# Cross-attention and BitLinear FFN: another order of loads, projections, squares and last steps

## The reference, cut to what matters

```
q = LN(x) @ Wq.T + bq;  k = ctx @ Wk.T + bk;  v = ctx @ Wv.T + bv
a = softmax(q k.T / 4, masks) @ v
x = x + a @ Wo.T + bo
h = gelu(silu(bitlinear(LN(x), w1, b1)))          # 512 -> 2048
h = (h - mean(h)) * rsqrt(var(h) + eps) * g + b
x = x + bitlinear(h, w2, b2)                      # 2048 -> 512
bitlinear(x, w, b): x rms-normed, scaled to +-127 per token and rounded; w -> {-1,0,1} * mean|w|
```

## Time and profile before

| stretch, us | what runs | PE | DVE | ACT | PE clock |
|---|---|---|---|---|---|
| 0 to 42 | start, up to the first score | 26.31 | 22.52 | 11.04 | 0.99 |
| 42 to 62 | first pass of batch 0 | 17.97 | 18.30 | 7.66 | 0.86 |
| 62 to 91 | body 0, second pass | 20.14 | 18.19 | 16.64 | 0.76 |
| 91 to 111 | body 0, first pass of batch 1 | 15.60 | 18.13 | 2.32 | 0.87 |
| 111 to 163 | body 1 up to its first pass | 41.52 | 29.06 | 26.27 | 0.85 |
| 189 to 436 | bodies 2 to 5 | 237.40 | 219.04 | 166.20 | 1.00 |
| 436 to 475 | body 6 up to its first pass | 31.25 | 32.84 | 23.28 | 0.87 |
| 498 to 552 | body 7 | 42.02 | 36.15 | 31.13 | 0.87 |
| 552 to 580 | body 8, first part | 20.79 | 23.08 | 21.84 | 1.00 |
| 580 to 621 | bodies 8 and 9, end | 25.37 | 28.60 | 10.82 | 0.75 |

### The profile page before, as it was taken

One profiled execution on the slowest core, in us unless ns is written; L12 is line 12 of the kernel. 1 busy time (PEld: TensorE's weight loads), 2 busy tenths in 40 slices (PEclk: granted clock), 3 DMA queues, 4 the chain that ended last, 5 costly groups with the idle time before them and its releaser, 6 DMA issues.

```text
span 620.8 us, 8914 instructions
## 1 busy us (share of the span) xinstructions
PE 524.9 (85%) x3374; PEld 289.5 (47%) x3374; DVE 489.0 (79%) x728; ACT 350.8 (57%) x424; POOL 135.0 (22%) x101
## 2 busy tenths in 40 slices
PE   4778497689889999999999999999869969698446
PEld 4666133362456355645564556455425523343222
DVE  3769939349699978997899789988896887648784
ACT  0244280517584867486748674867187739287630
POOL 5030031100611061106110611301140113103220
PEclk9989598797989999999999999999969989799688
DMA  8588637934422641365136412642134221100000
GB/s 315 152 234 324 211 84 191 386 116 146 86 67 105 183 99 36 125 195 114 36 124 191 102 54 76 191 98 74 40 86 102 74 75 17 38 0 1 34 34 35
DMA packets 32994, 72.17 MB, mean 116 GB/s; under 512 B 7167, under 2 KB 14529, under 8 KB 29950
## 3 DMA queue, kind: packets, MB, share of 16 engines
q1 hardware_dynamic: 31798, 71.26, 38.8%
q10 hardware_dynamic: 1152, 0.31, 0.2%
HBM read 46.50 MB, written 20.61 MB: 108 GB/s over the span
## 4 chain that ended last, share of the span: by engine, by line
PE 58%; DVE 12%; DMA 10%; ACT 9%; issue 7%; SPq 2%; POOL 1%; ACTq 1%; DVEq 0%
PE FF L853 9%; PE FF L678 7%; PE PV L792 7%; PE FF L901 6%; ACT PT L1069 5%; PE PV L775 5%; PE S L759 5%; PE S L735 5%; DVE negm L1337 4%; PE S L888 3%; PE FF L855 2%; PE PV L735 2%; DMA work<-in_w 2%; PE FF L867 2%; DMA num<-o_raw 2%
## 5 line engine op out<-in xcount | busy, mean ns | idle before, releaser
L1069 ACT ACTIVATE PT<-S 128x1024 f32<-128x1024 f32 x128 | 123.6, 1033 | 28.1 <-PE S L759 28.0
L1337 DVE TENSOR_REDUCE negm<-S 128x4 f32<-128x1024 f32 x88 | 105.6, 1215 | 24.7 <-PE S L735 23.2
L759 PE MATMUL S<-Q,K 100*128 100x512 bf16 x256 | 78.0, 413 | 27.7 <-ACT PT L1069 18.3
L775 PE MATMUL PV<-PT,vaug 128*32 128x256 f32 x1024 | 71.8, 400 | 0.4 <-ACT PT L1069 0.4
L853 PE MATMUL FF<-w1t,xqT 128*128 128x512 bf16 x256 | 67.4, 386 | 2.0 <-ACT PT L1100 1.1
L1100 ACT ACTIVATE work<-FF,s 128x512 f32<-128x512 f32 x56 | 38.5, 687 | 40.6 <-PE FF L855 40.6
L792 PE MATMUL PV<-wo_sb,num 128*128 128x512 f32 x128 | 59.9, 614 | 0.4 <-DVE negm L1337 0.4
L678 PE MATMUL FF<-xnT,wq_sb 128*128 128x256 f32 x224 | 52.8, 394 | 8.6 <-ACT xnT L1039 8.6
L735 PE MATMUL S<-K,Q 97*128 97x256 bf16 x352 | 54.5, 282 | 6.6 <-issue 3.5
L759 PEld LDWEIGHTS S<-Q,K 100*128 100x128 bf16 x256 | 18.7, 101 | 77.4 <-ACT PT L1069 54.8
L1337 DVE TENSOR_REDUCE negm<-PV 128x4 f32<-128x1024 f32 x40 | 48.8, 1221 | 6.3 <-PE PV L735 5.9
(11 more groups left out here) (196 smaller groups left out, 858.5 us busy)
## 6 DMA issues: line engine op xcount, KB each, us to landing
Q<-q_d SPq DMA_DIRECT2D x15, 768.0 KB
work<-in_w SPq DMA_DIRECT2D x8, 1024.0 KB, 11.4
q_d<-part SPq DMA_DIRECT2D x8, 768.0 KB, 3.6
x_sb<-in_x SPq DMA_DIRECT2D x8, 512.0 KB, 4.0
ctx_sb<-in_ctxT SPq DMA_DIRECT2D x8, 512.0 KB, 4.0
q_d<-part SPq DMA_DIRECT2D x8, 512.0 KB, 3.3
xb_sb<-in_x SPq DMA_DIRECT2D x8, 512.0 KB, 3.9
rec<-rec_d SPq DMA_DIRECT2D x30, 128.0 KB, 2.6
```

The lines of the kernel that those rows point to most:

```text
L759: last = pe.matmul(where, K[0:ROWS_2, g, kt * P:(kt + 1) * P], Q[0:ROWS_2, g, 2 * pair:2 * pair + 2, :], start=not masked, stop=True)
L775: last = pe.matmul(PV[32 * r:32 * r + 32, g % 4, :], vaug[:, c % 2, kt, g, :], PT[:, n % PT_SLOTS, r, :], start=(kt == 0), stop=(kt == TT ...
L1069: act.activation(PT[:, n % PT_SLOTS, :, :], ST[n % 2][:], ACT.Exp, scale=0.25).then_inc(S["pt_made"], 1)
L1337: dve.tensor_reduce(negm[:, t, R * g:R * g + R], RING_1[n % 3][:], AX.X, ALU.max, negate=True).then_inc(S["max_made"], 1)
```

## The change

All edits are made together:

- **Start.** On PE `project_kv` is split; K(0) comes first, then x(0) is turned, then V(0). ACT takes `keys`, `turned_x` and `values_in` in that order and K no longer waits for bv's load. On DVE `key_rests(0)` moves ahead of `masks`, and the first `maximum` ahead of `key_rests(1)`. On SP x(1) goes ahead of the second context, w1's chunk 0 behind `key_parts(0)`, x(2) from ahead of `query_parts(0)` to behind `rows_back_first`, w1's chunks 1 to 3 behind x(2).
- **w2.** GpSimd issues the four chunks on its own queue, as soon as w1_done, ahead of `norm_1(3)`. The sum, mean and first two DVE passes of w2 move forward in body 1; the third stays.
- **Bodies.** On PE `project_out(f, 0)`, `turn_max`, `turn_x(w)`, `project_out(f, 1)`, `project_q(w)`, K(a), the first two `scores_2`, V(a). The V copy follows the second exponential. In body 6 `squares(t, 1)` follows the second exponential. SP's `rows_back(a, 1)` goes ahead of the last denominators and numerators. The mean is an ACT instruction behind each gelu.
- **End.** In body 7 both `squares` go behind exponentials, `turn_hq` uses S1 and S0 instead of FF and needs no eviction first, and DVE takes `maximum_2(t, 1)` ahead of `turn_1`. In body 8 all of `layer_1` runs ahead of `layer_2_last(6, 1)`. In body 9 `shift(t, 0)` comes ahead of `spread_last(t, 1)`.

```
+
+def turned_hq_ps(t, n):
+    where = S0w if t == B - 3 and n > 1 else S1w
+    return where[:, 512 * (n % 2):512 * (n % 2) + 512]
...
 def weight_sum_ps(n):
-    return PV[:, 0, 0:1] if n == 0 else FF[:, 1, 1:2]
+    return PV[:, 0, 0:1] if n == 0 else S1[:, 0, 0:1]
...
         sp.dma_start(work[:, cols], w[:, cols]).then_inc(S[f"w_chunk{n}"], 16)
-
-    weight_chunk(w1, 0)
-    weight_chunk(w1, 1)
...
 
-    def second_weights():
-        sp.wait_ge(S["w1_done"], 1)
-        for n in range(4):
-            weight_chunk(w2, n)
+    def layer_rows():
         for to, of in ((b2_bc, b2), (g_bc, ln_g), (b_bc, ln_b)):
             sp.dma_start(to[:], of.partition_broadcast(P)).then_inc(S["w_two"], 16)
...
         if at_start(a):
+            load_x(1)
             load_context(1)
-            load_x(1)
             key_parts(0)
-            load_x(2)
+            weight_chunk(w1, 0)
             query_parts(0)
             negatives()
             rows_back_first()
-            weight_chunk(w1, 2)
-            weight_chunk(w1, 3)
+            load_x(2)
+            for n in range(1, 4):
+                weight_chunk(w1, n)
             query_parts(1)
             key_parts(1)
             weights_and_biases()
...
             denominators(c, 2)
-            denominators(c, 3)
-            numerators(c, 1)
         if a is not None:
             rows_back(a, 1)
         if c is not None:
+            denominators(c, 3)
+            numerators(c, 1)
+        if c is not None:
             reciprocals(c)
         if at_start(c):
-            second_weights()
+            layer_rows()
...
+    def second_weights():
+        pool.wait_ge(S["w1_done"], 1)
+        for n in range(4):
+            cols = slice(2048 * n, 2048 * n + 2048)
+            pool.dma_start(work[:, cols], w2[:, cols]).then_inc(S[f"w2_chunk{n}"], 16)
...
-
-    def mean_3(f, t):
-        pool.wait_ge(S["gelu_made"], 2 * f + t + 1)
-        tt(st[:, 1, t:t + 1], st[:, 0, t:t + 1], cst("-1/inner", (P, 1)), ALU.mult, "mu_made")
...
+        if at_start(c):
+            second_weights()
         if w is not None and w + 1 < B:
             norm_1(w + 1)
             norm_1_apply(w + 1)
...
-    def weight_sum(n, a):
-        if n == 0:
-            pe.wait_ge(S["max_made"], 16)
-        else:
-            pe.wait_ge(S["k_made"], a + 1)
-            pe.wait_ge(S["r1k_made"], a + 1)
-            pe.wait_ge(S["v_placed"], a + 1)
+    def weight_sum(n):
+        pe.wait_ge(S["max_made"], 16 * n + 16)
         pe.wait_ge(S["w_sum"], n + 1)
         pe.matmul(weight_sum_ps(n), ones[:], wsum[:, n:n + 1], start=True, stop=True
...
-    def project_kv(a):
+    def project_k(a):
         if at_start(a):
...
         for k in range(KD):
-            pe.matmul(to[:, 0:T], wkv_sb[:, k, 0:P], ctx_sb[:, k, :],
-                      start=(k == 0), stop=(k == KD - 1))
+            last = pe.matmul(to[:, 0:T], wkv_sb[:, k, 0:P], ctx_sb[:, k, :],
+                             start=(k == 0), stop=(k == KD - 1))
+        last.then_inc(S["k_ps"], 1)
+
+    def project_v(a):
+        if a == 1:
+            pe.wait_ge(S["v_placed"], 1)
+        to = pair_of(a)
         for t in range(TT):
             for k in range(KD):
                 last = pe.matmul(to[:, 512 + t * P:512 + (t + 1) * P],
...
+        if n == 1 and c == 1:
+            pe.wait_ge(S["w_mean"], 4)
         if n >= 2:
...
-        pe.wait_ge(S["hqT_made"], 4 * t + n - 1)
+        if t > B - 3:
+            pe.wait_ge(S["hqT_made"], 4 * t + n - 1)
         for k in range(8):
-            last = pe.transpose(S1w[:, 512 * half:512 * half + 512].bitcast(BF16)[:, k * P:(k + 1) * P],
+            last = pe.transpose(turned_hq_ps(t, n).bitcast(BF16)[:, k * P:(k + 1) * P],
...
     def body_of(c, a, f, t, masked):
         w = next_front(a) if c != 0 else None
-        if w is not None:
-            turn_x(w)
         if f is not None:
             project_out(f, 0, c)
         if c is not None:
             turn_max(c)
+        if at_start(c) or at_start(f):
+            weight_sum(c)
+        if w is not None:
+            turn_x(w)
+        if f is not None:
+            project_out(f, 1, c)
         if w is not None:
             project_q(w)
-        if f is not None:
-            project_out(f, 1, c)
         if a is not None and a > 1:
-            project_kv(a)
-        if at_start(c) or at_start(f):
-            weight_sum(c, a)
+            project_k(a)
         for g in range(G + 1):
             if c is not None and g < G:
                 scores_2(c, 2 * g, masked)
                 scores_2(c, 2 * g + 1, masked)
+            if g == 0 and a is not None and a > 1:
+                project_v(a)
             if c is not None and g > 0:
                 values(c, 2 * g - 2)
...
             for n in range(4):
-                turn_hq(t, n, f)
+                turn_hq_last(t, n)
             for n in range(4):
-                layer_1(f, n, t)
+                layer_1(f, n, None)
             project_out(c, 0, None)
             project_out(c, 1, None)
             for n in range(4, 8):
-                layer_1(f, n, t)
+                layer_1(f, n, None)
             layer_2_last(t, 0)
         elif f is not None:
             turn_xq_last(f)
-            layer_1(f, 0, None)
-            layer_1(f, 1, None)
+            for n in range(8):
+                layer_1(f, n, None)
             layer_2_last(t - 1, 1)
...
-    project_kv(0)
+    project_k(0)
     turn_x(0)
+    project_v(0)
     project_q(0)
     mask_flag()
     turn_x(1)
     project_q(1)
-    project_kv(1)
+    project_k(1)
+    project_v(1)
...
 def _(act):
-    act.dma_start(bk_sb[:], bk).then_inc(S["w_bias"], 16)
+    act.dma_start(bk_sb[:], bk).then_inc(S["w_bk"], 16)
...
-    def keys_and_values(a):
-        act.wait_ge(S["kv_ps"], a + 1)
+    def keys(a):
+        act.wait_ge(S["k_ps"], a + 1)
         wait_for(act, S["k_out"], 48 * a)
         if at_start(a):
-            act.wait_ge(S["w_bias"], 48)
+            act.wait_ge(S["w_bk"], 16)
         act.activation(part[:, 0, R, :], pair_of(a)[:, 0:T], ACT.Identity, bias=bk_sb[:, 0:1]
                        ).then_inc(S["k_made"], 1)
+
+    def values_in(a):
+        act.wait_ge(S["kv_ps"], a + 1)
         if at_start(a):
...
                        ).then_inc(S["gelu_made"], 1)
+        act.wait_ge(S["gelu_made"], 2 * f + t + 1)
+        act.activation(st[:, 1, t:t + 1], st[:, 0, t:t + 1], ACT.Identity, scale=-1.0 / INNER
+                       ).then_inc(S["mu_made"], 1)
...
-            squares(t, 0)
             act.activation(table_call[:, 1:2], table_call[:, 0:1], ACT.Exp)
             for n in range(16):
                 exps(c, n)
-                if n == 3:
-                    squares(t, 1)
+                if n in (1, 3):
+                    squares(t, n // 2)
...
-            keys_and_values(0)
-            for b in range(2):
-                turned_x(b)
-                queries(b, 0)
-                queries(b, 1)
-            keys_and_values(1)
-            weight_abs_sum(0, range(2))
+            keys(0)
+            turned_x(0)
+            values_in(0)
+            queries(0, 0)
+            queries(0, 1)
+            turned_x(1)
+            queries(1, 0)
+            queries(1, 1)
+            keys(1)
+            values_in(1)
             turned_x(2)
-            weight_abs_sum(0, range(2, 4))
+            weight_abs_sum(0)
...
@@ -1185,16 +1195,20 @@
         if w is not None:
             queries(w, 0)
             queries(w, 1)
-        if t is not None and a is not None:
+        if t is not None and w is not None:
             squares(t, 1)
         if c is not None:
 
             act.activation(table_call[:, 1:2], table_call[:, 0:1], ACT.Exp)
         if a is not None and a > 1:
-            keys_and_values(a)
+            keys(a)
         if c is not None:
             for n in range(16):
                 exps(c, n)
+                if n == 1 and w is None and t is not None:
+                    squares(t, 1)
+                if n == 1 and a is not None and a > 1:
+                    values_in(a)
                 if n in (5, 9, 13):
                     values_out(c, (n - 5) // 4)
...
         maximum_2(t, 0)
         power_2(t)
+        maximum_2(t, 1)
         turn_1(f)
-        maximum_2(t, 1)
+        reciprocal_last(c)
         factor_2(t)
         scale_2(t)
-        reciprocal_last(c)
         normalise_last(c, 0)
         normalise_last(c, 1)
         for n in range(4):
-            turn_2(t, n)
+            turn_2_last(t, n)
...
+        maximum_2(t, 0)
         residual_2(t - 1, 1)
-        maximum_2(t, 0)
         power_2(t)
...
         gain(t, 0)
+        shift(t, 0)
         spread_last(t, 1)
-        shift(t, 0)
         gain(t, 1)
         power_last(t, 0)
...
             norm_1_apply(0)
+            key_rests(0)
             masks()
-            key_rests(0)
             norm_1(1)
             norm_1_apply(1)
             query_rests(0)
```

(29 more changed lines are left out.)

26 lines of the change are left out of this document (9 added, 17 removed).

## The result

The changed kernel took **625.46 us** (median of 20 runs, 620.92 to 628.69) against 621.76 for the kernel before on the same chips: ratio 1.0054, 95% interval 1.0031 to 1.0076. The forecast was 614, with 621 as its upper end.

The account below looks back on a forecast made before the run. TensorE was taken as full in bodies 2 to 5, with waits movable in the start, body 1 and bodies 6 to 9. Terms 9.1 + 1.2 - 10 - 2.1 - 5.0 - 1.9 = -8.7 gave 613.9 from 622.6 (614.0 by median), range 604 to 621.

Parts of the forecast that it names:

- step 3: Second half rows ahead of denominators 3: reciprocal waits 2 to 3 in body 0; +1.2 us, bounds -1.1 and +3.5.
- step 5: Bodies 2 to 5: TensorE's earlier work taken back by ScalarE; 0, bounds -1 and +1.5 over four bodies.
- step 7: Body 7: scaling and turns end 2.1 sooner, project_out(7) at 540, not 545.01; -5.0 us, bounds -3 and -7.
- step 4: w2 issued early by GpSimd, there before body 1, whose scores_2(1,0) comes sooner; -10 us, bounds -8 and -11.
- rival C: w2 lands late from GpSimd's queue and holds body 1; 629 from a landing at 128.6; chance 0.12.
- Step 1: Start: K, turning x and V back to back, so Q(0) starts at 15.8 instead of 18.33.
- Step 2: Start: new wait for x(2), first score at 48.4, last maximum 71.1; +9.1 us with Step 1's gain contained.
- Step 6: Body 6: exponential 0 need not wait for squares(t, 1), VectorE next holds turn_xq; -2.1 us, bounds 0 and -5.
- Step 8: Bodies 8 and 9: deviations(7, 1) no longer wait 3.40, late residual costs 0.4; -1.9 us, bounds 0 and -3.
- A: Start: x(2) lands 6.3 or less behind its issue; 611.7 or lower, to 605; chance 0.19.
- B: Start: x(2) lands 11.8 behind its issue, +3.2 us, 617.2; chance 0.15.
- D: Denominators late by 1 to 1.5 us in each of six bodies; 620 to 622; chance 0.07.

Follow-up runs that it names:

- g2: The changed kernel unaltered, run and profiled again: ratio 1.0040 to the kernel before, profiled at 623.66 us.
- f3: Changed kernel with w2's issue, project_out(f,1) and x(2) put back, plus last denominators and numerators ahead of rows_back(a,1): 0.9811 of the kernel before.
- g1: The same file as f3, run and profiled again: 0.9802 of the kernel before.
- e4: Changed kernel with project_out(f,1) behind project_q(w) again: 0.9967 of the kernel before.
- e7: Changed kernel with w2's issue, project_out(f,1) and x(2) put back, plus V beside K again: 0.9787 of the kernel before.
- e5: Changed kernel with SP's load of x(2) ahead of w1's first chunk and query_parts(0): 0.9921 of the kernel before.
- e2: Changed kernel with the four w2 transfers back on SP's queue at the end of body 0: 0.9900 of the kernel before.
- e8: Changed kernel with VectorE's residual_1(f,1) ahead of maximum_2(t,0) in every body: 1.0053 of the kernel before.
- g4: f5 with VectorE's residual_1(f,1) ahead of maximum_2(t,0), as in e8: 0.9667 of the kernel before.
- f5: Changed kernel with w2's issue, project_out(f,1) and x(2) put back, plus body 7's first two silus between the last numerators' issues: 599.90 us, 0.9662.
- e3: Changed kernel with w2 on GpSimd's queue held until batch 0's four denominators transfers have landed: 0.9948 of the kernel before.

## Why the prediction was wrong, by its own steps

The forecast said 614.0 and the median is 625.46. Of these 11.5 us, 6.9 lie in the stages of the table (−1.8 for −8.7), and 4.5 are the distance of the profiled run from its own median, of which g2's profile shows 2.8. The stages missed both ways: +7.7 in step 3, +4.3 in step 5 and +3.2 in step 7, against −8.4 in the others together, so that by luck the sum is nearer than its terms.

**Step 3 failed**: "it would wait 2 to 3 in body 0, where w2 shares the engines. Taken +1.2". The mechanism was named and the place was right; the size was 9.89 us of waiting and +8.9 in the stage, outside its bound of +3.5. The landing was priced by a row in which the queue had the engines to itself. The two halves of the mechanism stood in two different steps: w2's landing, taken in step 4 as anything up to 107.3 on the clock of the kernel before, was not laid over the denominators' issue, which by the same clock falls near 92. The rule of the Trainium skill that the text set beside rival C ("DMA: Bandwidth & Descriptors", "Queues, rings and completion order": engines take packets in turn from the queues that have work) made it say "w2 would slow SP's transfers of body 0 instead of being late itself". The traces agree with its first half: 13.3 us for 8 KB beside w2, and no wait over 0.51 without it. But w2 was slowed too: its last sum begins 23.8 us after the issue (86.80 to 110.58), where the chunks took 14.0 on SP's queue. It should have been a rival with a price. And the order itself is a gain: with w2 away it is worth 8 us (f3, g1), in part by a way that step 3 did not see, the 32 KB behind the rows.

**Step 5 failed**: "0, bounds −1 and +1.5". It counted how long each engine would take and not that K writes where Q(w)'s rests are still read. In the kernel before, the second project_out lay between the earlier trace rows; the change moved that cover away. Measured +4.3. In it are 1.93 of waiting per body, and 1.0 to 1.7 us in each body where the clock falls behind it (body 4 takes 64.13 from project_out to project_out, body 3 62.45; body 5 takes 64.89 with the low clock and 63.85 in g2 without it). e4 gives 5.4 back, over bodies 1 to 5. Against this stands the hidden V, costed at nothing, which is worth 6.6 over bodies 1 to 6 (e7).

**Step 1 held**: Q(0) starts at 15.39 (15.8 forecast, 18.33 before).

**Step 2 was right in kind**, too high by 1.9 at the last maximum: x(2) issued 34.10 (forecast 36.4), landed 8.9 after issue (8.6), first score 46.47 (48.4), last maximum at 69.19 (71.1). SP was 2.3 earlier than reckoned. At body 0's scores only 5.8 of the 7.3 us are left, since these wait for the maxima's way through memory, 5.23 in the changed kernel. What the step could not tell is that its wait was needless: e5 takes it away and keeps the gain of step 1 at the first score. At the second pass it is gone in e5 too (72.46, 70.70 before): there the new start as a whole brings nothing, even without the wait.

**Step 4 was right**: −11.2 for −10, early passes and all; but its gain does not need GpSimd's queue. e2 has it with w2 issued at 108.9 by SP, where the sums hold VectorE for 3 us.

**Step 6** was right in sign and too small (−3.5 for −2.1). The hold that it named, VectorE ahead of turn_xq, did not come in the changed kernel (470.52, no wait). VectorE's residual did, with 1.85 in front of the first value step; e8 and g4 show no difference without it.

**Step 7 was mis-sized**, −1.8 for −5.0. TensorE's wait for VectorE's evictions did go. In its place came ScalarE's issue of the numerators: 4.66 us instead of 3.25, so that it ends as late after the start of the body as before (39.4 against 39.5), where the forecast had it end 2.1 sooner. TensorE waits 4.16 for the silu behind it, and its next tile runs at the low clock. Timeline of the changed kernel:

```profile
536.41 4.66 ACTq L1139 DMA_DIRECT2D num<-ctx_sb  x4
...
541.18 1.28 ACT L1104 ACT_TABLE_LOAD   x1 [6.87 <-issue]
...
543.22 1.89 PE L851 MATMUL FF<-w1t,xqT 128*128 128x512 bf16 x4 [4.16 <-ACT work L1104]
...
546.86 0.59 PE L791 MATMUL PV<-wo_sb,num 128*128 128x512 f32 x1
```

f5, which moves two silus ahead of half of this issue, shows that the issue was the hold of project_out(7).

**Step 8** gained 3.7 for 1.9. The wait of deviations for GpSimd is gone, as forecast; what the rest of the gain is was not taken apart.

The rivals: A, B and C hung on landings that were foreseen well; none held. D named the denominators' stall, but in all bodies instead of one. The case that came, one long stall in body 0 by w2 and a hold of K in each body, was in no rival.

## What to carry to other kernels

A large load moved earlier onto another queue can lie under every small transfer that is issued before it has landed, as w2 did here: list those and ask which in-order engine stands behind each. When a step of TensorE is moved, look at what used to lie between two steps that share a PSUM bank, since that step was also the cover of the evictions. Undo parts one at a time before judging a change by its sum: here three bad ones (23 us) hid all the good ones. And when a part brings a gain, ask whether it needs its whole edit: body 1's gain came from the order of the sums and passes, and stayed when w2's load went back to SP's queue.

## What the runs showed of the hardware that I had not expected

- 8 KB issued by SP behind 0.96 MB of its own and into a 4.2 MB load from GpSimd's queue took 13.3 us to land, 64 KB 11.6 (2.8 with the same 0.96 MB but without the load, in e2).
- A TensorE wait of 1.93 us in otherwise full work was followed by the low clock in some bodies and not in others of the same run (bodies 4 and 5, not 3), at 1.0 to 1.7 us each time.
- A VectorE operation on 128x2 elements took 2.22 us instead of 0.16, begun 0.15 us after a GpSimd addition of 2.35 us, and TensorE waited 1.80 for the chain behind it (timeline of e4, body 5). e3 has two more such operations, shown above.

```profile
407.32 2.35 POOL L488 TENSOR_TENSOR xb_sb<-xb_sb,bo_bc 128x1024 f32<-128x1024 f32 x1 [1.88 <-DMA xb_sb<-in_x]
407.47 2.22 DVE L1446 TENSOR_TENSOR s<-s,inv 128x2 f32<-128x2 f32 x1
...
410.16 0.28 PE L815 MATMUL FF<-identb,inv 128*128 128x128 bf16 x2 [1.80 <-DVE inv L1450]
```
